# A row of ones from the relu, transposes between two output tiles, and norms moved, in an eight-layer attention kernel with a routed expert gate

## What is computed

```python
xn = _layernorm(x, axis=-1)
s = _L0_attn_ref(xn, ...)        # 8 layers, 16 heads of 8
g = _silu(_L0_ffn_ref(xn, ...))  # one of 8 experts for each sequence
x = x + s * g
...
# a layer of the attention branch
q, k = phi(h @ wq + bq), phi(h @ wk + bk)          # phi = elu + 1
kv = einsum('bshd,bshm->bhdm', k, v)
z = 1 / (einsum('bshd,bhd->bsh', q, k.sum(axis=1)) + 1e-06)
h = ln(h + (q kv z) @ wo + bo); h = ln(h + gelu(h @ w1 + c1) @ w2 + c2)
...
# the expert branch, e the expert chosen for a sequence
y = relu(zn @ W_down[e] + b_down[e]) @ W_up[e] + b_up[e]; y = y * gate
```

## Time and profile before

| | |
|---|---|
| median of 3 runs | 852.19 us (851.09 to 852.88) |
| the profiled execution | 852.55 us, its span 850.8 us |
| PE busy | 806.7 us (95%) |
| PE weight loads | 734.9 us (86%) |
| DVE busy | 764.9 us (90%) |
| ACT busy | 735.8 us (86%) |
| POOL busy | 415.2 us (49%) |
| granted PE clock, mean | 0.983 |

### The profile page before, as it was taken

One profiled execution on the slowest core, in us unless ns is written; L12 is line 12 of the kernel. 1 busy time (PEld: TensorE's weight loads), 2 busy tenths in 40 slices (PEclk: granted clock), 3 DMA queues, 4 the chain that ended last, 5 costly groups with the idle time before them and its releaser, 6 DMA issues.

```text
span 850.8 us, 19233 instructions
## 1 busy us (share of the span) xinstructions
PE 806.7 (95%) x5914; PEld 734.9 (86%) x5914; DVE 764.9 (90%) x2670; ACT 735.8 (86%) x1315; POOL 415.2 (49%) x395
## 2 busy tenths in 40 slices
PE   5698999999999999999999999999999999999993
PEld 3588899989999999999999999999999998988862
DVE  5888998999999898999899898998999898999877
ACT  2479999988999899988999899998999899989875
POOL 5243444454544454544454444444454454456667
PEclk9789999999999999999999999999999999999996
DMA  5300200101010100101010000101000000000002
GB/s 149 90 2 1 45 1 2 35 2 44 2 35 2 45 2 1 35 2 45 1 27 11 25 20 2 35 2 45 1 21 16 1 2 2 1 20 8 1 14 87
DMA packets 26264, 18.76 MB, mean 22 GB/s; under 512 B 4354, under 2 KB 22195, under 8 KB 26164
## 3 DMA queue, kind: packets, MB, share of 16 engines
q1 hardware_dynamic: 25300, 16.95, 7.2%
q10 hardware_dynamic: 864, 0.59, 0.2%
HBM read 15.43 MB, written 2.10 MB: 21 GB/s over the span
## 4 chain that ended last, share of the span: by engine, by line
PE 80%; DVE 9%; ACT 6%; issue 3%; POOL 1%; DMA 0%; POOLq 0%; ACTq 0%; DVEq 0%
PE down_ps L759 21%; PE att_ps L720 7%; PE small_ps L690 6%; PE up_ps L749 5%; PE up_ps L751 5%; PE up_ps L750 5%; PE t_ps L668 5%; PE t_ps L727 4%; PE kq_ps L680 3%; PE kq_ps L681 3%; PE kq_ps L682 3%; DVE z_lo L1044 3%; ACT z_hi L914 2%; PE up_ps L711 2%; PE small_ps L698 2%
## 5 line engine op out<-in xcount | busy, mean ns | idle before, releaser
L759 PE MATMUL down_ps<-w_use,hid 128*128 128x128 f32 x2048 | 259.5, 275 | 0.7 <-ACT hid L865 0.7
L759 PEld LDWEIGHTS down_ps<-w_use,hid 128*128 128x128 f32 x2048 | 243.8, 192 | 2.7 <-ACT hid L865 2.7
L1062 POOL TENSOR_TENSOR res_ffn<-z_tm,g_ffn 128x512 f32<-128x512 f32 x64 | 81.9, 1279 | 241.2 <-DVE k_e L1175 235.9
L1051 POOL TENSOR_TENSOR res_att<-z_tm,g_att 128x512 f32<-128x512 f32 x64 | 82.5, 1288 | 155.1 <-DVE h L1002 155.1
L865 ACT ACTIVATE hid<-up_ps 128x512 f32<-128x512 f32 x192 | 113.4, 592 | 22.2 <-PE up_ps L751 14.7
L1014 DVE BATCH_NORM_STATS2 st<-h 128x6 f32<-128x128 f32 x504 | 107.5, 276 | 0.1
L920 ACT ACTIVATE z_tm<-h,shift,rstd 128x128 f32<-128x128 f32 x248 | 101.5, 482 | 1.3 <-DVE shift L1031 1.3
L749 PE MATMUL up_ps<-z_hi,w_hi 128*128 128x512 f32 x192 | 86.4, 450 | 2.2 <-ACT hid L865 1.7
L1065 POOL TENSOR_TENSOR res_ffn<-res_ffn,ffn_row 128x512 f32<-128x512 f32 x64 | 84.0, 1313 | 5.0
L1054 POOL TENSOR_TENSOR res_att<-res_att,att_row 128x512 f32<-128x512 f32 x64 | 82.3, 1286 | 5.0
L680 PE MATMUL kq_ps<-w_kq_hi,zq_hi 128*128 128x256 f32 x256 | 82.0, 320 | 1.5 <-DVE zq_lo L957 1.5
(11 more groups left out here) (223 smaller groups left out, 1966.4 us busy)
## 6 DMA issues: line engine op xcount, KB each, us to landing
raw_w<-in_L_attn_W SPq DMA_DIRECT2D x15, 256.0 KB, 4.6
out_y<-gate_tm SPq DMA_DIRECT2D x8, 256.0 KB, 2.2
bias_bc<-in_L_attn_c SPq DMA_DIRECT2D x7, 256.0 KB, 4.8
x_tm<-in_L_attn_x SPq DMA_DIRECT2D x3, 512.0 KB, 7.8
raw_rows<-in_L_attn_be SPq DMA_DIRECT2D x15, 64.0 KB, 4.3
raw_g<-in_L_attn_g SPq DMA_DIRECT2D x14, 64.0 KB, 3.2
x_tm<-in_L_attn_x SPq DMA_DIRECT2D x2, 256.0 KB, 3.5
raw_rows<-in_L_attn_bo SPq DMA_DIRECT2D x8, 64.0 KB, 3.9
```

The costliest lines, as they stand in the source:

```text
L759: last = nc.tensor.matmul(down_ps[:, t, :], hid[:, j, t * P:(t + 1) * P], w2_use[:, j, :], start=(j == 0), stop=(j == FC - 1))
```

## The change

- e_hid loses its memset. The down product gets a 65th column of zeros (ew_down) and the relu's bias a 65th row of one (eb_down), so the relu writes the row of ones. Two memsets on POOL set these, with a wait between them; the constants are 13 and no longer 12. The wait for them goes from the first up product to the first down product and the first relu of the experts. The DMAs of W_down and b_down write to the first 64 columns and rows.
- act_final_norm is cut in two: tiles 0 and 1 come right after the exponential of the next unit's queries, tiles 2 and 3 stay at the end of the period.
- Behind the last period, PE does the z1 transposes of unit 63 between output tiles 2 and 3 of unit 62.
- dve_last_affine is cut in two. The first half (gain) of sequence 6 comes ahead of the addition of unit 63, that of sequence 7 ahead of the second tail shift, the second halves come after.
- L1251, a tensor_scalar with two constants, becomes a subtraction of two tensors, ones - tl_m.

```diff
--- before.py
+++ after.py
@@ -320,8 +320,9 @@
         wr_sb = sb("wr_sb", [P, E])
         br_bc = sb("br_bc", [SEQS, E])
         expert_i = sb("expert_i", [SEQS, 1], I32)
-        ew_down = sb("ew_down", [P, SEQS, HID])
-        eb_down = sb("eb_down", [HID, SEQS])
+
+        ew_down = sb("ew_down", [P, SEQS, HID + 1])
+        eb_down = sb("eb_down", [HID + 1, SEQS])
         ew_up = sb("ew_up", [HID + 1, SEQS, D])
         e_hid = sb("e_hid", [HID + 1, SEQS, S])
         st_x = sb("st_x", [P, SEQS * TT, 6])
@@ -355,7 +356,7 @@
         tl_r = sb("tl_r", [P, 7 * TT])
         tl_m = sb("tl_m", [P, 7 * TT])
         tl_sh = sb("tl_sh", [P, 7 * TT])
-        CONSTS, CONSTS_EARLY = 12, 6
+        CONSTS, CONSTS_EARLY = 13, 6
 
 
 
@@ -589,20 +590,22 @@
                 pe.wait_ge(s["z1lo_s"], UNITS)
             elif i == 7:
                 pe.wait_ge(s["gelu"], (UNITS - 1) * FC + 3)
-            nc.tensor.matmul(e_down_bank[i][0:HID, :], ew_down[:, w, :], zf_fm[:, w, :], start=True, stop=True).then_inc(s["e_down"], 1)
+            if i == 0:
+                pe.wait_ge(s["const_ready"], CONSTS)
+            nc.tensor.matmul(e_down_bank[i][0:HID + 1, :], ew_down[:, w, :], zf_fm[:, w, :], start=True, stop=True).then_inc(s["e_down"], 1)
 
         def act_expert_relu(act, i):
             w = EXPERTS[i]
             act.wait_ge(s["e_down"], i + 1)
-            nc.scalar.activation(e_hid[0:HID, i, :], e_down_bank[i][0:HID, :], ACT.Relu,
+            if i == 0:
+                act.wait_ge(s["const_ready"], CONSTS)
+            nc.scalar.activation(e_hid[:, i, :], e_down_bank[i][0:HID + 1, :], ACT.Relu,
                                  bias=eb_down[:, w:w + 1]).then_inc(s["e_hid_s"], 1)
 
         def pe_expert_up(pe, i):
             w = EXPERTS[i]
             pe.wait_ge(s["e_hid_s"], i + 1)
-            if i == 0:
-                pe.wait_ge(s["const_ready"], CONSTS)
-            elif i == 1:
+            if i == 1:
                 pe.wait_ge(s["h1_s"], UNITS)
             if i < TANH:
                 pe.wait_ge(s["ew_scaled"], i + 1)
@@ -922,8 +925,9 @@
 
 
 
-        def act_final_norm(act, w):
-            for t in range(TT):
+        def act_final_norm(act, p, w, tiles):
+            act.wait_ge(s["shift_s"], p)
+            for t in tiles:
                 i = 2 * TT + t
                 nc.scalar.activation(z_tm[:, w, t, :], z_tm[:, w, t, :], ACT.Identity, scale=rstd[:, i:i + 1],
                                      bias=shift[:, i:i + 1]).then_inc(s["zf_n"], 1)
@@ -974,6 +978,8 @@
                 behind_keys()
             if proj:
                 act_q_exp(act, p + 1)
+            if fin and p < UNITS - 1:
+                act_final_norm(act, p, p - 5 - FIRST_LAST, (0, 1))
             if p == UNITS - 1:
                 act_expert_relu(act, 0)
                 act_norm2(act, p, (b - 3) % SEQS)
@@ -988,7 +994,7 @@
             if ln2 and p < UNITS - 1:
                 act_norm2(act, p, (b - 3) % SEQS)
             if fin and p < UNITS - 1:
-                act_final_norm(act, p - 5 - FIRST_LAST)
+                act_final_norm(act, p, p - 5 - FIRST_LAST, (2, 3))
             if between:
                 between()
 
@@ -1205,13 +1211,16 @@
             nc.vector.tensor_tensor(tail_ps[u - FIRST_LAST][:, :, :], down_ps[:, :, :], res_ffn[:, u % 2, :, :],
                                     ALU.add).then_inc(s["h2_s"], 1)
 
-        def dve_last_affine(dve, w, slot):
+        def dve_last_gain(dve, w, slot):
             bank = tail_ps[w]
             dve.wait_ge(s["tl_mv_s"], TT * (slot + 1))
             for t in range(TT):
                 i = slot * TT + t
                 nc.vector.scalar_tensor_tensor(bank[:, t, :], bank[:, t, :], tl_mv[:, i, 0:1], fin_bc[:, 0, :],
                                                ALU.subtract, ALU.mult).then_inc(s["last_c"], 1)
+
+        def dve_last_scale(dve, w, slot):
+            bank = tail_ps[w]
             dve.wait_ge(s["last_c"], TT * (w - 5))
             for t in range(TT):
                 i = slot * TT + t
@@ -1248,7 +1257,7 @@
             c = slice(first * TT, last * TT + TT)
             nc.vector.tensor_tensor(tl_m[:, c], tl_mv[:, c, 0], tl_r[:, c], ALU.mult).then_inc(s["tl_mr_s"], 1)
             dve.wait_ge(s["tl_mr_s"], calls)
-            nc.vector.tensor_scalar(tl_sh[:, c], tl_m[:, c], -1.0, 1.0, ALU.mult, ALU.add).then_inc(s["tl_sh_s"], 1)
+            nc.vector.tensor_tensor(tl_sh[:, c], ones[:, c], tl_m[:, c], ALU.subtract).then_inc(s["tl_sh_s"], 1)
 
         def dve_final_norm(dve, w):
             dve.wait_ge(s["shift_s"], UNITS - 1)
@@ -1403,8 +1412,8 @@
                 sp.wait_ge(s["routed"], 1)
                 for b in range(SEQS):
                     e = sp.value_load(expert_i[b:b + 1, 0:1], min_val=0, max_val=E - 1)
-                    sp.dma_start(ew_down[:, b, :], W_down[bass.ds(e, 1)].rearrange("a d h -> d (a h)")).then_inc(expert_in[b], 16)
-                    sp.dma_start(eb_down[:, b:b + 1], b_down[bass.ds(e, 1)].rearrange("a h -> h a")).then_inc(expert_in[b], 16)
+                    sp.dma_start(ew_down[:, b, 0:HID], W_down[bass.ds(e, 1)].rearrange("a d h -> d (a h)")).then_inc(expert_in[b], 16)
+                    sp.dma_start(eb_down[0:HID, b:b + 1], b_down[bass.ds(e, 1)].rearrange("a h -> h a")).then_inc(expert_in[b], 16)
                     sp.dma_start(ew_up[0:HID, b, :], W_up[bass.ds(e, 1)].rearrange("a h d -> h (a d)")).then_inc(expert_in[b], 16)
                     sp.dma_start(ew_up[HID:HID + 1, b, :], b_up[bass.ds(e, 1)]).then_inc(expert_in[b], 16)
 
@@ -1445,8 +1454,10 @@
                 pool_w2(pool, 0, False)
                 pool_period(pool, 0, 1)
                 pool.wait_ge(s["t2m"], 2)
-                nc.gpsimd.memset(e_hid[HID:HID + 1, :, :], 1.0).then_inc(c, 1)
+                nc.gpsimd.memset(eb_down[HID:HID + 1, :], 1.0).then_inc(c, 1)
                 pool.wait_ge(c, 11)
+                nc.gpsimd.memset(ew_down[:, :, HID:HID + 1], 0.0).then_inc(c, 1)
+                pool.wait_ge(c, 12)
                 nc.gpsimd.iota(expert_m8[:, :], pattern=[[1, E]], base=-E, channel_multiplier=0,
                                allow_small_or_imprecise_dtypes=True).then_inc(c, 1)
                 pool.wait_ge(c, CONSTS)
@@ -1492,8 +1503,9 @@
                 last = UNITS - 1
                 pe_up(pe, last - 1, UNITS, range(FC))
                 pe_expert_down(pe, 1)
-                pe_down(pe, last - 1, range(TT))
+                pe_down(pe, last - 1, (0, 1, 2))
                 pe_z1_transpose(pe, last, UNITS)
+                pe_down(pe, last - 1, (3,))
                 pe_expert_up(pe, 1)
                 pe_up(pe, last, UNITS, range(FC))
                 pe_down(pe, last, range(TT))
@@ -1624,16 +1636,18 @@
                 dve_tail_stats(dve, S_F4, z_tm[:, 4], s["y_s"], 5)
                 dve_tail_stats(dve, S_W6, small_ps, s["h2_s"], p - 1)
                 dve_expert_gate(dve, 1)
+                dve_last_gain(dve, 6, S_W6)
                 dve_h2_tail(dve, last)
 
                 dve.wait_ge(s["tl_r_s"], 1)
                 dve_tail_shift(dve, S_F3, S_F4, 1)
                 dve_tail_stats(dve, S_W7, down_ps, s["h2_s"], p)
                 dve_tail_stats(dve, S_F5, z_tm[:, 5], s["y_s"], 6)
-                dve_last_affine(dve, 6, S_W6)
+                dve_last_scale(dve, 6, S_W6)
+                dve_last_gain(dve, 7, S_W7)
                 dve.wait_ge(s["tl_r_s"], 2)
                 dve_tail_shift(dve, S_F5, S_F5, 2)
-                dve_last_affine(dve, 7, S_W7)
+                dve_last_scale(dve, 7, S_W7)
                 dve_tail_stats(dve, S_F6, small_ps, s["y_d"], TT)
                 dve_tail_stats(dve, S_F7, down_ps, s["y_d"], 2 * TT)
 
```

## The result

The changed kernel took **845.88 us** (median of 4, 844.92 to 846.95) against 852.01 (851.09 to 852.88) for the kernel before on the same chip: a ratio of 0.9929 [0.9911, 0.9946]. The forecast was 846.8, within 844.7 to 849.6, and faster at 0.93.

A forecast was written before the change was run, and what follows sets the result against it. PE was taken to bound the whole span, with gains only at the start and in the tail: 3.0 + 1.15 + 0.4 + 1.05 = 5.6 us off 852.55 or the median, 846.95 or 846.6; said 846.8, range 844.7 to 849.6.

The forecast's parts named there:

- The row of ones: At the start, removing POOL's 3.50 us e_hid memset frees DVE's L194 and gains 3.0 us.
- The step from the memset to L194: Near 20.36 us, L194 is held while POOL's memset writes; without it, it takes 0.15 instead of 3.24 us.
- The step from L194 to PE: From L194 to PE's first query transposes DVE is the chain, so nearly all of the 3.07 us passes.
- PE's clock: At the start, half rate behind PE's idle: 1.7 us more gained if it stays full, 1.5 lost if half lasts; taken as 0.
- The norms: In units 62 and 63, moving two of four norms into ACT's idle time gains 1.15 us, range 0 to 1.54.
- den_e loses to POOL: Rival: in unit 62 den_e arrives too late for POOL's boundary; the norms gain 0.5 or 0, 847.4 to 848; chance 0.18.
- The transposes: Before unit 63's first up product, PE's z1 transposes moved ahead of tile 3 gain 0.4 us, range 0.2 to 0.64.
- The last affine: Near the end, four instructions moved into DVE's 2.72 us of idle before unit 63's addition gain 1.05 us.
- The subtraction: In the tail shift, subtracting two tensors on DVE waits for POOL just as tensor_scalar did: gain 0.
- the subtraction passes POOL: Rival: the tail shift's subtraction is not held by POOL; 0.4 us more gain, 846.4; chance 0.06.
- The 65th row: Rival: the experts' products or relus of 65 rows go in two passes, costing 6.3 us, 852.9 to 853.5; chance 0.03.
- The change doesn't do what it says: Rival: at the start, L194 was held by something other than the memset, so 3 us stay, 849.8; chance 0.03.

The follow-up runs named there:

- e3: The changed kernel with the old e_hid memset put back in its old place, ahead of the two small ones: 848.52 us.
- e1: The kernel before with the row of ones alone (e_hid memset out, 65th column and bias row in): 848.32 us, ratio 0.9960.
- e2: The kernel before with the same e_hid memset issued earlier, where POOL waits for a DMA, no 65th row: 847.79 us, ratio 0.9953.
- e7: The changed kernel with the tail shift as a tensor_scalar again, one execution: 846.01 us.
- e8: The changed kernel with the tail shift computed on ACT instead of DVE, one execution: 842.57 us.
- e5: The changed kernel with the z1 transposes of unit 63 back behind all 32 down products, one execution: 845.81 us.
- e9: e8 plus POOL's affines moved later and the final norm of sequence 2 moved from DVE to ACT: 842.41 us, ratio 0.9892 to the kernel before.
- e4: The changed kernel with all four final norms together at the end of ACT's period again, one execution: 847.36 us.
- e6: The changed kernel with each first half of the last affine back right ahead of its second half, one execution: 845.06 us.
- e10: The changed kernel again, unedited, on another chip beside e9: 845.38 us, ratio 0.9926 to the kernel before.

## Why the prediction was right

Point by point, by its own steps.

**The row of ones, 3.0 forecast.** The step from the memset to L194 held: e3 brings the stall back with the memset, and e1 and e2 take it away without the rest of the change. The step from L194 to PE held to the hundredth: from L194's start to PE's first query transposes it is 29.64 - 20.36 = 9.28 us before, and 27.38 - 21.17 = 6.21 after and in the seven other traces in which L194 takes 0.17, which is the 3.07 of the forecast. But in the profiled pair the transposes came only 2.26 earlier, at 27.38 and not near 26.6, because L194 itself began 0.81 later than before (the last section says what its start varies with).

What made up for that goes with PE's clock, which the forecast took at 0 with bounds of -1.7 to +1.5; the bounds were needed. Before, and in e3 and e7, the query transposes ran at half rate, behind 2.69, 2.69 and 1.30 us in which PE had no work, and from them to the first z_hi it took 12.56, 13.88 and 13.63 us; in the nine other traces they ran at full rate, and it took 10.88 to 11.37. In the pair that is 12.56 - 11.21 = 1.35 more gained. The half rate did not go away with the stall, though. Before it was granted from 26.8 to 33.7 us and from 40.5 to 47.3; after, from 18.4 to 25.2 and from 38.9 to 45.7. Busy time of PE, PEld, DVE, ACT and POOL, granted clock, DMA share and GB/s in two stretches after:

```profile
20.00:24.00 4.00, 3.53 (x17) 3.26 (x16) 3.29 (x17) 0.00 (x0) 0.00 (x0) 0.50 0.01 2
...
38.90:45.70 6.80, 6.15 (x27) 5.47 (x26) 6.37 (x30) 3.37 (x5) 2.54 (x2) 0.50 0.08 23
```

So after the change PE runs at half for 6.8 us behind the first z_hi, where it was 5.1 before, and in that stretch 0.87 goes back. Over the twelve traces the two go together: with 2.4 to 3.3 us at half behind the first z_hi (e3, e7, e8) it takes 709.35 to 709.52 us from there to z_hi of unit 58, with 4.8 to 5.6 (before and five others) 709.99 to 710.57, and with 6.8 (the change, e5, e9) 711.00 to 711.38. No run changed the clock by itself.

So the 2.74 of the profiled pair is 3.07 - 0.81 + 1.35 - 0.87. The steps on DVE and PE were right; that the other three nearly cancel is luck. By whole runs the term is 3.3 (e1), 3.8 (e2), and 2.6 to 3.1 by putting the memset back (e3).

**The norms, 1.15 forecast, 1.25 measured**, by the profiled pair and by e4. The course was the forecast one, den_e passing at the boundary and m_r held to the end of the next POOL instruction, in both units. Rival "den_e loses to POOL" (0.18) fell: den_e started 0.01 us before L1057's end, L1060 0.09 after den_e's start. The margin is small, but den_e had it in each of the seven traces with the split norms and POOL's order of the change (0.08 to 0.10). That row is the near race that no row of before had shown. It also bears on the rule that the prediction quotes (the Trainium skill, "SBUF — State Buffer", "Who interferes with whom": whoever issues first holds the shared pair for the whole instruction). The trace agrees in unit 62, by 784.28 against 784.37. In unit 63 it adds what the rule leaves out: an instruction of DVE that waits gets in between two of POOL's that stand back to back. And e3 does not fit it as the records have it: L194 starts 0.02 ahead of the memset and is held for all of it. Whether it really issued first is not shown.

**The transposes, 0.4 forecast**: 0.37 in the pair, 0.26 by e5; inside 0.2 to 0.64. The pair's figure holds 0.11 that came with the 65th column (e1 and e5), so 0.26 is the better size of the edit. The 0.1 that I added for a full pipe was not seen by itself.

**The last affine, 1.05 forecast**: 1.16 in the pair, 1.18 by e6. I took the 1.03 of the four instructions themselves; what was removed from the path is 0.1 more, and POOL's slack (1.48, now 0.30, so 1.18 used) covered it, as forecast.

**The subtraction, 0 forecast**: e7 shows 13.93 with either form. Rival "the subtraction passes POOL" fell. What POOL's slack would let through was right too: e8, in which the wait truly is gone, gained 0.36 of the 0.4 that I let POOL's slack pass, and turned POOL into the bound.

**The 65th row** fell by the rows of 1.04 and 0.67: what it would have cost was 6.3 us, and e1 and e2 are 0.5 apart, with intervals that overlap. I took its cost at 0, at most 0.06 for each expert; it gained 0.2 in the stretch between units 62 and 63, which the forecast did not see. "The change doesn't do what it says" fell by L194.

That the sum, 5.6, met the profiled pair's 5.6 is partly luck as well: the start was 0.26 under its term and the other terms 0.26 over theirs, 0.2 of it by the 65th column. Over whole runs the gain is 6.1 and 6.3 us, 0.5 to 0.7 more than the sum, and the 846.8 lies 0.9 above the median measured. The four terms by their experiments are 3.3 (e1) + 1.25 + 0.26 + 1.18 = 6.0. That would put the start above its 3.0, but the interval of the first gain, 4.6 to 7.6 us, and that of e1, 2.2 to 4.6, are too wide to tell.

Of what I named as signs of being wrong, two came near: POOL's last wait fell to 0.30, against my bound of 0.2, and the early offset was 2.26 at the query transposes and 2.70 two units behind the first z_hi, against 3.

## What to carry to other kernels

A stall between DVE and POOL is priced first by where the two instructions meet. If they meet, DVE's can be held for what is left of POOL's, however short it is itself; if they don't, POOL's length costs nothing. Moving the same memset to POOL's idle time (e2) gained as much as removing it (e1), and giving POOL's queue an order that leaves DVE's short chained instructions free (e9) gained another 3 us, some 0.4 of it from the shift on ACT. When one of them is freed, look at which reader comes to the next boundary: here m_r took over a part of what den_e had lost. An edit that changes how long PE waits can also change its clock, in that stretch and in later ones, so a stall taken away at one place is followed through the granted clock to the steady state. An edit in the first 50 us is measured by several whole runs; one in the tail by a distance inside the trace, since the start of a single execution moved by up to 4 us.

## What the runs showed of the hardware that was not expected

- **The start is not the same twice.** In nine profiles with nothing large in L194's way and POOL's late order as in the change or before, z_hi of unit 60 lies between 770.98 and 774.97, though apart from e2 their code for the first 50 us is the same. What their traces show to differ is when the first DMAs land, how POOL and DVE then meet, and where PE ran at half rate (the mean granted clock from 18 to 36 us was 0.81 in the changed kernel's first profile and 1.00 in its second, e10). From the timelines of DVE, before and then after:

```profile
11.95 1.34 DVE L396 TENSOR_SCALAR z_tm<-x_tm,r_x,shift_x 128x128 f32<-128x128 f32 x4
```

```profile
11.90 3.27 DVE L397 TENSOR_SCALAR z_tm<-x_tm,r_x,shift_x 128x128 f32<-128x128 f32 x4
```

  And of POOL in the changed kernel:

```profile
9.83 0.46 POOL L273 TENSOR_TENSOR row_sum<-raw_rows 128x128 f32<-128x128 f32 x1 [6.21 <-DMA raw_rows<-in_L_attn_c]
...
11.80 1.28 POOL L1057 TENSOR_TENSOR res_att<-z_tm,g_att 128x512 f32<-128x512 f32 x1
```

  POOL could take its rows at 9.83 instead of 11.43, so its L1057 began at 11.80, just ahead of DVE's four norms, which took 3.27 us instead of 1.34. The twelve traces bear it out: where POOL began on the rows at 9.88 us or earlier (six of them) the norms took 2.22 to 3.44, where it began at 10.29 or later (the other six) 1.25 to 1.49. A DMA that lands earlier made DVE slower. In the profiled pair the delay is still there at DVE's k_phi (17.64 against 16.83), and it is the 0.81 by which L194 came later.
- **A memset on POOL cost by the length of its rows, not by how many partitions it writes.** 1x4096 took 3.50 us; the two that replace it, 1x8 and 128x8, took 0.10 and 0.11, and 128x128 took 0.20 (raw_g, at 3.28 us).
- **A memset that only writes holds a DVE tensor_scalar of four columns for its whole length**, also when DVE is recorded as starting 0.02 us ahead of it (e3).
- **DVE's hold was followed by PE's half rate.** Where L194 was held for 0.8 us or more (before, e3, e7), PE had no work for 1.30 to 2.69 us and then ran its query transposes in 1.11 to 1.12 us instead of 0.66; in the nine other traces it did not.
